# Dealing half of the node blocks over the turns of the gather passes of a graph network

## The chip, the cores and the metric

The kernel runs on one core of one Trainium2 chip. Five engines work beside one another, each through its own instructions in order: TensorE (PE), VectorE (DVE), ScalarE (ACT), GpSimd (POOL) and SyncE (SP), which here only issues transfers. They meet through semaphores. The metric is the device time of one execution, in microseconds (us); lower is better. Before the change three runs took 4184.45, 4190.33 and 4193.7 us.

## The reference, cut to what matters

There are 100,000 nodes of 128 features and 25,000 edges sorted by target. Four graph layers follow one another, each with a layer norm of its residual sum. The last one is a Chebyshev layer in two convolutions, with a ReLU between them. Cut to its chain:

```python
x = _layernorm(x + _L0_gnn_ref(x, edge_attr, ...))       # segment sum of edge attributes, two matmuls, softplus
x = _layernorm(x + _L1_gnn_ref(x, edge_weight, ...))     # own rows @ W_self.T + mean of neighbours @ W_neigh.T
x = _layernorm(x + _L2_gnn_ref(x, w_s, w_n, ...))        # relu(x @ w_s + sum of neighbours @ w_n)
x = _layernorm(x + _L3_gnn_ref(x, W1, b1, W2, b2, ...))  # h = relu(cheb(x)); cheb(h); lap() gathers edges twice in each
```

With so few edges most nodes are nobody's target. A node without an incoming edge goes through the four layers by dense arithmetic alone. The nodes that are targets need gathered rows of their sources at each layer.

## The kernel before, in words

**Stages.** Ten stages follow one another, and at each border every engine drains, adds to the semaphore `seam` (`leave`) and waits for all five (`enter`). They are a preparation (degrees, folded weights, a node table), `tgt0` and `src0` (the first layer for the rows of edge targets and the dense path for the rows of edge sources), `nodes`, then the five gather passes `L1`, `L2`, `T1`, `T2`, `LH`, and a last pass `LU`, which scatters the corrected rows over the output.

**The stage nodes** takes all 100,000 rows in 196 blocks (`BLOCKS`) of 512 rows, each held as 128 partitions by 4 by 128 values, through the four layers without neighbours. Its turn `g` works on six blocks at different depths. SP loads `xin` (`x_load`). POOL adds a constant row (`make_y0`, L599) and looks up two columns of a node table with two indirect transfers (L647). PE transposes `y0` (L1383), multiplies it by `A1` (L1527), and DVE makes `y1` of it (L1023). PE transposes `y1`, multiplies by `ws_sb` (L1533), DVE makes `u2` (L1037). POOL makes `x3 = (u2 - mean) * rs` in four instructions (L622) and `x3b = x3 + gb2_row` in one (L609). PE transposes `x3`, multiplies it by `G02` (L1547), ACT makes the hidden rows `hT` with ReLU (L1273), PE multiplies by `V02` (L1540), DVE adds `x3b` to get `y3` (L1043), and ACT normalizes it into `outb` (L1307), which SP stores. DVE takes moments with `bn_stats` and `bn_aggr` (L969, L974) of `y0`, `u2` and `y3`; ACT takes square roots (L1142) and the sums of squares of `y1` (L1286), and carries the transposed tiles from PSUM to SBUF (L1137).

**A gather pass** has 49 turns (`QUADS`), each over 512 edges: POOL gathers their source rows with four indirect transfers (L563), ACT weighs them, PE transposes them (`sums`, L1401), DVE adds up runs of equal targets with a scan (L853), and PE multiplies the result by the weights of that layer (`first`, `second`). `L1` and `L2` end with a layer norm on DVE; `T1`, `T2` and `LH` are the three steps of the Chebyshev layer. The sums have two PSUM banks, and the products another two to four.

**What orders the work** is the written order of instructions on each engine, and the waits written into it; nothing is planned at run time. In both programs all loops are unrolled.

Of the kernel before, what the change touches and what calls it, by code (L numbers as in the profile page):

```python
# [12 lines left out]
P = 128  # L28
# [14 lines left out]
RING = 4  # L43
assert TILES == 4 * QUADS and QUADS % 2 == 1 and BLOCKS % 2 == 0

# [64 lines left out]
def gnn_kernel(nc, x, src, dst, attr, ew, W1, b1, W2, b2, Wself, bself, Wneigh, bneigh, ws, wn, G1, gb1, G2, gb2, out):  # L110
    ctx = ExitStack()
    with ctx:
# [54 lines left out]
        xin, y0, y1, u2, x3, x3b, outb = (sb(n, [P, 2, 4, P]) for n in ("xin", "y0", "y1", "u2", "x3", "x3b", "outb"))  # L167
# [10 lines left out]
        lk = sb("lk", [P, 2, 4])  # L178
# [4 lines left out]
        pre_in = (y0, x3b, xin, outb)  # L183
# [9 lines left out]
        SELF, NEIGH = (5, 3), (7, 6)  # L193
        HALVES = ((6, 7), (3, 5))
        FIRST = (5, 7)

# [11 lines left out]
        LATE = {"tgt0": 3, "L1": 1, "L2": 1, "T1": 1, "T2": 1, "LH": 1, "LU": 1}  # L208
# [5 lines left out]
        def transfer(name, at_once=2, **n):  # L214
# [6 lines left out]
        x_in = transfer("x_in", nodes=1)  # L221
        xe_in = transfer("xe_in", RING, L1=1, L2=1, T1=1, LH=1, LU=1)
        pre_arrived = transfer("pre_arrived", RING, T2=1)
# [4 lines left out]
        look_in = transfer("look_in", nodes=2)  # L228
        out_st = transfer("out_st", tgt0=1, src0=1, nodes=1)
        oe_st = transfer("oe_st", RING, L1=1, L2=1, T1=1, T2=1, LH=1)  # L230
        more_st = transfer("more_st", src0=1, T1=1, T2=1, LH=1)
# [5 lines left out]
        x3b_made = signal("x3b_made", "nodes")  # L237
# [3 lines left out]
        y3_made, bn3, mv3, rs3, off3_made, looked_up = (  # L241
            signal(n, "nodes") for n in ("y3_made", "bn3", "mv3", "rs3", "off3_made", "looked_up"))
# [11 lines left out]
        out_made = signal("out_made", "tgt0 nodes L1 L2 LH LU")  # L254
# [4 lines left out]
        sd1, h_kept = signal("sd1", "src0"), signal("h_kept", "src0 T2")  # L259
        sd3 = signal("sd3", "nodes")  # L260
        hidden = signal("hidden", {"nodes": 2, "T2": 1})
# [7 lines left out]
        y0_turned, p1_made, y1_turned, p2_made, x3_turned, h_made = (  # L269
            signal(n, "src0 nodes") for n in ("y0_turned", "p1_made", "y1_turned", "p2_made", "x3_turned", "h_made"))  # L270
# [6 lines left out]
        h_turned = signal("h_turned", "T2")  # L277
# [44 lines left out]
        spb, = (yTc[:, n, :] for n in range(1))  # L322
# [3 lines left out]
        LOADS, EDGE_LOADS = 15, 12  # L326
        COUNTED = [c for c in range(TILES) if c % 3 == 0]
        PUT = [c for c in range(TILES) if c % 3 != 0]
        V_COLS, V_WEIGHTS, V_BTC, V_TABLE = 1, 2, 3, 4
        T_TURNED, T_FOLDED, T_A1, T_COUNTED = 1, 2, 3, 4  # L330
# [5 lines left out]
        def _(sp):  # L336
# [6 lines left out]
            with nc.allow_non_contiguous_dma("edge lists with an edge per partition; columns of biases"):  # L343
# [15 lines left out]
                for t, s in ((b1_col, b1), (bs_col, bself), (bn_col, bneigh)):  # L359
                    load(t[:, :], s.rearrange("(p a) -> p a", a=1))  # L360
# [16 lines left out]

            def edge_pass(p, state=None, store=None):
                def state_load(g):
                    if state is None or not g.inside(QUADS):  # L380
                        return
                    if p in ("L1", "T1"):
                        turned.wait(sp, p, g, back=RING)
                    if p == "L2":
                        step.wait(sp, p, g, back=RING)
                    if p == "LH":
                        out_made.wait(sp, p, g, back=RING)
                    if p == "LU":
                        step.wait(sp, p, g, back=RING, k=2)
                    sp.dma_start(xe[:, g.r], quad_of(state, g)).then_inc(xe_in.of(g), 16)  # L390

                def more_load(g):
                    if not g.inside(QUADS):
                        return
                    if p == "T2":
                        pre_added.wait(sp, p, g, back=RING)
                        sp.dma_start(flat(pre_in[g.r]), one(h_pre, g)).then_inc(pre_arrived.of(g), 16)
                    if p == "LU":
                        step.wait(sp, p, g, back=2, k=3)
                        sp.dma_start(gb_in[:, g.b], quad_of(state3, g)).then_inc(x3_in.of(g), 16)  # L400

                def turn(g):
                    state_load(g.less(-3))
                    more_load(g.less(-3 if p == "T2" else -1))
                    g = g.less(LATE[p])
                    if not g.inside(QUADS):
                        return
                    if p == "T1":
                        lap_kept.wait(sp, p, g)
                    elif p == "T2":  # L410
                        near_kept.wait(sp, p, g)
                    elif p != "LU":
                        out_made.wait(sp, p, g)
                    if store is not None:
                        sp.dma_start(quad_of(store, g), oe[:, g.r]).then_inc(oe_st.of(g), 16)
                    if p == "T1":
                        pre_kept.wait(sp, p, g)
                        sp.dma_start(one(h_pre, g), hb[:, g.b].rearrange("p k d -> p (k d)")).then_inc(more_st.of(g), 16)
                    if p == "T2":
                        h_kept.wait(sp, p, g)  # L420
                        sp.dma_start(quad_of(state_h, g), hb[:, g.b]).then_inc(more_st.of(g), 16)
                    if p == "LH":
                        u_kept.wait(sp, p, g)
                        sp.dma_start(quad_of(lap2, g), y1[:, g.b]).then_inc(more_st.of(g), 16)

                enter(sp, p)
                for c in range(3):
                    state_load(Turn(c))
                for c in range(3 if p == "T2" else 1):
                    more_load(Turn(c))  # L430
                run_turns(QUADS, LATE[p], turn)
                if store is not None:
                    oe_st.wait_all(sp, p)
                if p in more_st.n:
                    more_st.wait_all(sp, p)
                leave(sp)

# [58 lines left out]
            def x_load(g):  # L496
                if g.inside(BLOCKS):
                    y0_made.wait(sp, "nodes", g, back=2)
                    sp.dma_start(xin[:, g.b], block_of(x, g)).then_inc(x_in.of(g), 16)

            def nodes_turn(g):
                x_load(g.less(-2))
                g5 = g.less(5)
                if g5.inside(BLOCKS):
                    out_made.wait(sp, "nodes", g5)
                    if g5.c == BLOCKS - 1:
                        out_st.wait(sp, "nodes", g5, back=1)
                    sp.dma_start(block_of(out, g5), outb[:, g5.b]).then_inc(out_st.of(g5), 16)

            enter(sp, "nodes")  # L510
            x_load(Turn(0))
            x_load(Turn(1))
            run_turns(BLOCKS, 5, nodes_turn)
            out_st.wait_all(sp, "nodes")
            leave(sp)

            edge_pass("L1", state1, store=state2)
            edge_pass("L2", state2, store=state3)
            edge_pass("T1", state3, store=lap1)
            edge_pass("T2", store=near_out)  # L520
            edge_pass("LH", near_out, store=most_out)
            edge_pass("LU", most_out)

# [1064 lines left out]
```

## Time and profile before

| | |
|---|---|
| timed runs, us | 4184.45, 4190.33, 4193.7 |
| profiled execution, span from first to last instruction, us | 4620.6 |
| busy PE, DVE, ACT, POOL in that span, us | 3327.5, 3081.8, 2499.0, 3172.0 |
| mean granted clock of TensorE | 0.861 |
| stage nodes, us from the start | 1072 to 2481 |
| the five gather passes, us from the start | 2481 to 4055 |
| last pass, us from the start | 4055 to 4621 |

The times give no separate figure for the profiled execution, so its span stands for its own time. It lies 430 us above the median of the three runs, which were taken without a profile. So a share of what the profile shows is not in the metric, and which share is a question of its own. Busy time of TensorE is modelled at its end points; a gap between two instructions of an engine is shown in brackets with what released the engine.

### The profile page before, as it was taken

The page shows a single profiled execution, that of the slowest core. Times are in us where ns is not written, and L with a number is a line of the kernel's source. Part 1 is how long each engine was busy: PE and PEld are TensorE (multiplying, and loading weights), DVE is VectorE, ACT ScalarE, POOL GpSimd, SP SyncE. Part 2 cuts the span into 40 slices and gives each one's busy share as a digit, 9 for nine tenths or more (in the row PEclk, how much of TensorE's full clock was granted, in tenths as well). Part 3 has the DMA queues.
Part 4 walks back from the last instruction along what each step waited for, and adds up shares of the span by engine and source line. Part 5 has one row for each costly group of instructions (what it writes and reads, how often), then busy time and mean ns, then how long its engine had stood idle before and what let it go on. Part 6 is the DMA issues. An engine that isn't in the chain of part 4 may idle for free.

```text
span 4620.6 us, 74892 instructions
## 1 busy us (share of the span) xinstructions
PE 3327.5 (72%) x20670; PEld 2626.7 (57%) x20670; DVE 3081.8 (67%) x12829; ACT 2499.0 (54%) x7360; POOL 3172.0 (69%) x3630
## 2 busy tenths in 40 slices
PE   2278977778999999999995665658878878821111
PEld 0135646666888888888884654654446667721111
DVE  2298979997888888888885775761224434554454
ACT  0005768996888888888884552115546633311110
POOL 6506668876888888888885665656656646567676
PEclk6598989998999999999997787878989989955555
DMA  0005645662222222222222443435657756632222
GB/s 21 4 1 173 184 133 182 215 216 97 79 75 79 75 79 75 79 75 79 75 79 77 130 131 107 137 123 195 226 192 267 268 195 211 206 109 89 87 91 70
DMA packets 311878, 575.84 MB, mean 125 GB/s; under 512 B 69502, under 2 KB 97975, under 8 KB 311466
## 3 DMA queue, kind: packets, MB, share of 16 engines
q1 hardware_dynamic: 235178, 443.56, 28.5%
q0 software_dynamic: 76288, 127.51, 10.3%
q8 instruction: 171, 2.80, 0.3%
q14 instruction: 241, 1.97, 0.1%
HBM read 301.23 MB, written 271.14 MB: 124 GB/s over the span
## 4 chain that ended last, share of the span: by engine, by line
DVE 42%; issue 17%; PE 15%; another core or an unknown queue 11%; POOL 7%; ACT 5%; DMA 1%; DVEq 0%; SPq 0%; POOLq 0%; ACTq 0%; PEldq 0%; PEld 0%
DVE bn L969 11%; DVE y L1023 5%; DVE mv L974 4%; PE ps L1444 4%; POOL rows L563 3%; DVE u L1037 3%; DVE y L1043 3%; DVE x L853 2%; POOL out_dram L678 2%; PE ps L1383 2%; DVE bn L861 2%; DVE x3b L853 1%; PE ps L1401 1%; PE ps L1462 1%
## 5 line engine op out<-in xcount | busy, mean ns | idle before, releaser
L563 POOL DMA_INDIRECT rows<-state,rows_of_src x588 | 555.8, 945 | 378.6 <-issue 161.7
L853 DVE TENSOR_TENSOR_SCAN x<-same,x,ps 128x512 f32<-128x512 uint8 x336 | 428.8, 1276 | 303.8 <-remote 176.4
L1401 PE MATMUL ps<-ident,rows 128*128 128x128 f32 x1372 | 288.9, 317 | 438.6 <-ACT rows L1154 239.5
L1137 ACT ACTIVATE yTa<-ps 128x512 f32<-128x512 f32 x392 | 232.9, 594 | 567.7 <-PE ps L1383 295.5
L563 POOL DMA_INDIRECT rows<-lap,rows_of_lap x392 | 383.4, 978 | 210.1 <-issue 110.3
L1401 PEld LDWEIGHTS ps<-ident,rows 128*128 128x128 f32 x1372 | 203.6, 166 | 492.0 <-issue 304.7
L647 POOL DMA_INDIRECT lk<-node_table,look_idx x392 | 388.5, 991 | 91.9 <-issue 82.2
L1154 ACT ACTIVATE rows<-rows,lap_w 128x128 f32<-128x128 f32 (+1 forms) x784 | 269.8, 419 | 287.1 <-DMA rows<-lap,rows_of_lap 232.0
L1142 ACT ACTIVATE sd<-mv,consts 128x4 f32<-128x4 f32 x588 | 174.6, 297 | 438.7 <-DVE mv L865 163.8
L1540 PE MATMUL ps<-V,hT 128*128 128x128 f32 x3136 | 405.1, 283 | 8.4 <-ACT hT L1273 8.4
L969 DVE BATCH_NORM_STATS2 bn<-y 128x6 f32<-128x128 f32 x1764 | 378.7, 276 | 23.2 <-POOL y L599 23.1
L1540 PEld LDWEIGHTS ps<-V,hT 128*128 128x128 f32 x3136 | 367.6, 193 | 45.7 <-ACT hT L1273 42.0
L622 POOL TENSOR_SCALAR x<-u,negm,rs 128x128 f32<-128x128 f32 x784 | 339.5, 441 | 72.5 <-issue 61.3
L1547 PE MATMUL ps<-yTc,G 128*128 128x512 f32 x784 | 369.3, 593 | 1.9 <-ACT yTc L1137 1.9
L599 POOL TENSOR_TENSOR y<-xin,c0h 128x512 f32<-128x512 f32 x245 | 311.1, 1270 | 38.3 <-DMA xin<-in_x_dram 28.6
L1307 ACT ACTIVATE outb<-y,off,rs 128x128 f32<-128x128 f32 x784 | 322.5, 491 | 6.6 <-DVE off L999 6.6
L1383 PE MATMUL ps<-ident,x 128*128 128x128 f32 x1372 | 233.2, 298 | 124.3 <-DVE y L949 115.6
L1383 PEld LDWEIGHTS ps<-ident,y 128*128 128x128 f32 x1960 | 232.6, 143 | 148.8 <-issue 131.3
L1527 PE MATMUL ps<-A,yTa 128*128 128x128 f32 x1960 | 283.4, 288 | 34.2 <-ACT yTa L1137 24.1
L1286 ACT ACTIVATE unused<-y 128x128 bf16<-128x128 f32 x980 | 289.6, 310 | 0.0
L1383 PE MATMUL ps<-ident,y 128*128 128x128 f32 x1960 | 260.0, 276 | 38.8 <-POOL y L599 36.3
L1023 DVE SCALAR_TENSOR_TENSOR y<-ps,rs,b1c 128x128 f32<-128x128 f32 x980 | 276.0, 344 | 13.8 <-issue 2.6
(269 smaller groups left out, 9346.5 us busy)
## 6 DMA issues: line engine op xcount, KB each, us to landing
state_h<-hb SPq DMA_DIRECT2D x98, 512.0 KB
xin<-in_x_dram SPq DMA_DIRECT2D x196, 256.0 KB
out_dram<-outb SPq DMA_DIRECT2D x196, 256.0 KB
xe<-state SPq DMA_DIRECT2D x147, 256.0 KB
state<-outb SPq DMA_DIRECT2D x98, 256.0 KB
state<-oe SPq DMA_DIRECT2D x98, 256.0 KB
h_pre<-hb SPq DMA_DIRECT2D x49, 512.0 KB
rows<-in_edge_attr_10x_dram SPq DMA_DIRECT2D x48, 320.0 KB
```

The costliest lines, as they stand in the source:

```text
L563: gp.indirect_dma_start(out=dest[:, at, k, 0:width], out_offset=None, in_=table_, in_offset=bass.IndirectOffsetOnAxis(ap=index[:, c:c + 1] ...
L599: gp.tensor_tensor(y0[:, g.b], xin[:, g.b], all4(c0h[:, :]), ALU.add).then_inc(y0_made.sem, 1)
L622: i = gp.tensor_scalar(x3[:, g2.b, k, :], u2[:, g2.b, k, :], negm[:, g2.b, k:k + 1], rs[:, 2, g2.b, k:k + 1], ALU.add, ALU.mult)
L647: gp.indirect_dma_start(out=lk[:, g.b, 2 * j:2 * j + 2], out_offset=None, in_=node_table, in_offset=bass.IndirectOffsetOnAxis(ap=look_idx[ ...
L853: v.tensor_tensor_scan(t[0:np_, g.b].rearrange("p k d -> p (k d)"), same[0:np_, 512 * g.c:512 * g.c + 512], ps[0:np_, bk + g.b, :], t[0:np ...
L969: i = v.bn_stats(bn[:, n, k, :], y[:, k, :])
L1023: i = v.scalar_tensor_tensor(y1[:, g.b, k, :], bank(3)[:, k, :], dev(0, g.b, k), b1c[:, :], ALU.mult, ALU.add)
L1307: i = a.activation(outb[:, g5.b, k, :], y3[:, g5.b, k, :], ACT.Identity, bias=off3[:, g5.b, k:k + 1], scale=rs[:, 3, g5.b, k:k + 1])
L1383: i = t.transpose(bank(bk)[:, k, :], source[:, k, :], ident[:, :])
L1401: i = t.transpose(bank(g.b)[:, k, :], rows[:, g.r, k, 0:P], ident[:, :])
L1540: i = t.matmul(bank(7)[:, k, :], hT[:, j, k, :], V02[:, j, :], start=j == 0, stop=j == 1)
L1547: i = t.matmul(ps[:, 5 + j, :], G02[:, j * P:(j + 1) * P], yTc[:].rearrange("p k d -> p (k d)"), start=True, stop=True)
```

## The change

- The stage `nodes` handles only the first 98 blocks (`ALONE`). Each block's work on each engine is cut into three parts (`PARTS`): part 0, 1 and 2 of turn `g` are the numbers `3g`, `3g+1`, `3g+2`. In `nodes` the parts run one after another.
- The other 306 parts are dealt over the five gather passes. Four run at each border, before the engines wait for `enter` (on POOL between the first gathers). The 57 or 58 others of a pass run one after nearly each turn, on every engine (`Plan.after`). 286 of them are dealt over the 49 + 2 to 4 turns of the passes, four to seven turns of a pass having two.
- A gather pass keeps one PSUM bank for sums instead of two, one or two for products, and one for transposes, and the dealt parts share banks 0, 4, 5 and 6. Each pass lags its steps by more turns (`TAIL`).
- POOL no longer scales `u2`. DVE makes `x3 = u2 * rs + gb2_row` in four `scalar_tensor_tensor` instructions, and the mean is taken out by multiplying with centred weights (`G02c`), with a corrected bias column (`gb1c_col`). `negm` and the copy of the looked-up columns fall away on DVE. The look-ups (two columns for each of the 98 blocks) write `looked` directly.
- The four-deep ring `xin`, a few new tiles, two small matmuls and one load in the preparation.

The constants, and the parts on VectorE where it matters here:

```diff
+ALONE = BLOCKS // 2
+PARTS = 3
+SHARE = {"L1": 57, "L2": 57, "T1": 57, "T2": 57, "LH": 58}
...
+                if part == 0:
+                    if g.inside(n):
                         y0_made.wait(dve, p, g)
                         stats(0, y0[:, g.b], bn0)
+                    if g1.inside(n):
+                        p2_made.wait(dve, p, g1)
+                        y1_made.wait(dve, p, g1)
+                        v.scalar_tensor_tensor(u2[:, g1.b], bank(4), 0.0, y1[:, g1.b], ALU.max, ALU.add)\
+                            .then_inc(u2_made.sem, 1)
...
+                if part == 2:
+                    if g1.inside(n):
+                        sd2.wait(dve, p, g1)
...
+                        for k in range(4):
+                            i = v.scalar_tensor_tensor(x3[:, g1.b, k, :], u2[:, g1.b, k, :], dev(2, g1.b, k), gb2_row[:, :],
                                                        ALU.mult, ALU.add)
```

Between these, part 0 goes on with the moments of `y0` and `u2`, part 1 makes `y1` of the block `g` and takes the moments of the `y3` of block `g3`, and part 2 ends with `y3` of block `g2`. On ScalarE, parts 1 and 2:

```diff
+                if part == 1:
+                    if g1.inside(n):
+                        root(p, g1, sd2, tv2, sd[:, 2, g1.b, :], tmpv[:, g1.b, :], EPS2)
+                    if g2.inside(n):
+                        p3_made.wait(act, p, g2, back=1)
+                        for j in range(2):
+                            h_made.wait(act, p, g2, k=j + 1)
+                            a.activation(hT[:, j], bank(5 + j), ACT.Relu, bias=gb1c_col[:, j:j + 1])\
+                                .then_inc(hidden.sem, 1)
                     if g3.inside(n):
+                        root(p, g3, sd3, mv3, sd[:, 3, g3.b, :], mv[:, 2, g3.b, :, 1], EPS1)
+                if part == 2:
+                    if g4.inside(n):
+                        off3_made.wait(act, p, g4)
...
+                        i.then_inc(final_made.sem, 1)
+                    if g.inside(n):
+                        keep(p, g, y1T_kept, y1_turned, [(p2_made, 1)], yTb[:, :, :], 0 if shared else 1)
```

The `outb` instructions (L1307 before) stand at the dots of part 2. Part 0 copies the transposed `y0` and `x3` out of PSUM, takes the sums of squares and one root. Every gather pass deals the parts, on each engine, as here on VectorE:

```diff
+                for q in PLAN.seam[p]:
+                    node_part(q)
                 enter(dve, p)
+                for c in range(QUADS + TAIL[p]):
+                    turn(Turn(c))
+                    for q in PLAN.after(p, Turn(c)):
+                        node_part(q)
+                leave(dve)
```

On PE the parts are: part 0 transposes `y0` and the `x3` of two blocks back and multiplies the last block's `y1` by `ws_sb` (in the stage `nodes` the two transposes come first); part 1 multiplies `y0` by `A1` and the `x3` of two blocks back by `G02c`; part 2 transposes `y1` and multiplies `hT` by `V02`.

## Rows read from the trace of the kernel before

**Rows 1.** By stage: us, busy PE, PEld, DVE, ACT, POOL, clock, DMA share, GB/s.

```profile
1072.00:2481.00 1409.00, 1380.15 (x9408) 1133.40 (x9408) 1219.89 (x7272) 1193.63 (x3921) 1214.41 (x1568) 0.99 0.25 75
2481.00:2800.00 319.00, 192.75 (x1176) 179.48 (x1176) 215.75 (x735) 162.62 (x490) 184.94 (x196) 0.78 0.40 122
2800.00:3109.00 309.00, 187.17 (x1176) 174.47 (x1176) 214.26 (x735) 43.09 (x98) 186.35 (x197) 0.79 0.41 126
3109.00:3418.00 309.00, 251.75 (x980) 139.74 (x980) 62.64 (x49) 167.73 (x392) 184.49 (x196) 0.93 0.63 209
3418.00:3730.00 312.00, 255.42 (x1568) 196.79 (x1568) 118.21 (x98) 179.37 (x343) 184.91 (x196) 0.94 0.72 248
3730.00:4055.00 325.00, 255.99 (x1960) 242.94 (x1960) 152.20 (x147) 107.96 (x245) 185.28 (x196) 0.88 0.63 199
```

**Rows 2.** Busy time in the middle of the stage nodes.

```profile
1400.00:1854.00 454.00, 454.00 (x3119) 373.64 (x3118) 399.27 (x2402) 394.76 (x1299) 401.48 (x520) 1.00 0.25 77
```

**Rows 3.** Timeline of PE in nodes: start, us, what, count.

```profile
1800.08 1.14 PE L1527 MATMUL ps<-A,yTa 128*128 128x128 f32 x8
1801.05 1.11 PE L1533 MATMUL ps<-ws_sb,yTb 128*128 128x128 f32 x8
1802.16 2.05 PE L1540 MATMUL ps<-V,hT 128*128 128x128 f32 x16
1804.05 1.88 PE L1547 MATMUL ps<-yTc,G 128*128 128x512 f32 x4
1805.77 1.04 PE L1383 MATMUL ps<-ident,y 128*128 128x128 f32 x8
1806.64 0.60 PE L1383 MATMUL ps<-ident,x 128*128 128x128 f32 x4
1807.08 1.14 PE L1527 MATMUL ps<-A,yTa 128*128 128x128 f32 x8
```

**Rows 4.** Timeline of DVE in the same block.

```profile
1802.51 0.18 DVE L1014 RECIPROCAL rs<-sd 128x4 f32<-128x4 f32 x1
1802.72 1.13 DVE L1023 SCALAR_TENSOR_TENSOR y<-ps,rs,b1c 128x128 f32<-128x128 f32 x4
1803.77 0.68 DVE L1037 SCALAR_TENSOR_TENSOR u<-ps,y 128x512 f32<-128x512 f32 x1
1804.96 0.86 DVE L969 BATCH_NORM_STATS2 bn<-u 128x6 f32<-128x128 f32 x4
1808.10 0.38 DVE L974 BATCH_NORM_AGGREGATE mv<-bn 128x2 f32<-128x6 f32 x4
```

**Rows 5.** Timeline of ACT in the same block.

```profile
1799.41 0.60 ACT L1137 ACTIVATE yTa<-ps 128x512 f32<-128x512 f32 x1 [0.75 <-PE ps L1383]
1800.17 0.30 ACT L1142 ACTIVATE sd<-mv,consts 128x4 f32<-128x4 f32 x1 [0.17 <-DVE mv L974]
1804.01 1.64 ACT L1307 ACTIVATE outb<-y,off,rs 128x128 f32<-128x128 f32 x4
```

**Rows 6.** A group of POOL in the stage nodes: busy us, mean ns, idle before.

```profile
L599 POOL TENSOR_TENSOR y<-xin,c0h 128x512 f32<-128x512 f32 x196 | 248.9, 1270 | 28.7 <-DMA xin<-in_x_dram 28.6
```

**Rows 7.** Timeline of POOL at the border of L1 and L2.

```profile
2800.05 0.94 POOL L563 DMA_INDIRECT rows<-state,rows_of_src  x1 [25.22 <-SPq L291]
2801.30 0.94 POOL L563 DMA_INDIRECT rows<-state,rows_of_src  x1 [0.30 <-issue]
```

**Rows 8.** Waits of POOL in L1, then L2 (total us, times, longest).

```profile
POOL rows L563 <- remote: 19.7, 10, 3.6
POOL rows L563 <- remote: 38.3, 20, 3.7
```

**Rows 9.** Timeline of L2 around one of these waits.

```profile
2950.32 0.69 DVE L940 SCALAR_TENSOR_TENSOR y<-ps,xe 128x512 f32<-128x512 f32 x1 [2.03 <-remote]
2950.61 0.94 POOL L563 DMA_INDIRECT rows<-state,rows_of_src  x1 [1.64 <-remote]
```

**Rows 10.** Timeline of PE in T1 behind a gap.

```profile
3231.72 1.79 PE L1444 MATMUL ps<-yTa,G 128*128 128x512 f32 x2 [1.86 <-issue]
```

More of the change, by code:

```diff
@@ L376, in _ @@
             leave(sp)
[L378 to L436, printed above, removed]
@@ L497, in x_load @@
                 if g.inside(BLOCKS):
[L498 to L508, printed above, removed]
+                    y0_made.wait(sp, "nodes", g, back=RING)
@@ L510, in _ @@
             enter(sp, "nodes")
[L511 to L514, printed above, removed]
+            for c in range(3):
+                x_load(Turn(c))
+            for q in range(PARTS * ALONE):
+                node_part(q)
             leave(sp)
[L517 to L520, printed above, removed]
@@ L652, in _, with merged_pass, rows_of @@
+            assert TILES == 2 * ALONE
             enter(pool, "nodes")
             make_y0("nodes", Turn(0))
-            run_turns(BLOCKS, 4, row_pass("nodes", BLOCKS, look))
+            for q in range(PARTS * ALONE):
+                node_part(q)
             leave(pool)
-            def edge_pass(p, table_, index, width=P):
+            def merged_pass(p, table_, index, width=P):
+                def rows_of(g):
+                    if g.inside(QUADS):
+                        gather(p, g, table_, index, rows, g.r, width, rows_in, [(summed, RING)])
@@ new lines, in squares, with node_part @@
+            def squares(p, g):
+                y1_made.wait(act, p, g)
+                tv2.wait(act, p, g, back=2)
+                squared.wait(act, p, g, back=1)
+                for k in range(4):
+                    i = a.activation(unused[:, k, :], y1[:, g.b, k, :], ACT.Square, accum_out=ssum[:, g.b, k:k + 1])
+                i.then_inc(squared.sem, 1)
+            enter(act, "src0")
+            run_turns(QUADS, 5, src0_turn)
+            leave(act)
+            def node_part(q):
+                p, n = "nodes", BLOCKS
+                g, part = Turn(q // PARTS), q % PARTS
+                g1, g2, g3, g4 = (g.less(k) for k in (1, 2, 3, 4))
+                shared = q >= PARTS * ALONE
+                if part == 0:
@@ L1523, in turn @@
-                    if g.inside(n):
-                        y0T_kept.wait(pe, p, g)
-                        y1_made.wait(pe, p, g, back=1)
-                        for k in range(4):
-                            i = t.matmul(bank(3)[:, k, :], yTa[:, k, :], A1[:, :], start=True, stop=True)
-                        i.then_inc(p1_made.sem, 1)
+                    if not shared:
+                        third_turned()
                     if g1.inside(n):
@@ L1531, in turn @@
                         u2_made.wait(pe, p, g1, back=1)
-                        for k in range(4):
-                            i = t.matmul(bank(4)[:, k, :], yTb[:, k, :], ws_sb[:, :], start=True, stop=True)
-                        i.then_inc(p2_made.sem, 1)
-                    if nodes and g4.inside(n):
-                        hidden.wait(pe, p, g4)
-                        y3_made.wait(pe, p, g4, back=1)
+                        if shared and g3.inside(n):
+                            y3_made.wait(pe, p, g3)
```

982 lines of the change are left out of this document (706 added, 276 removed).

## The prediction

> **What bounds the kernel now.** I read the stages first, then one stage's timeline, then the waits.
>
> The busy times by stage [rows 1] split the part that changes into the stage nodes, 1409 us, and five gather passes of 309 to 325 us, 1574 us together; the sum is 2983 of the 4620.6 us of the profiled span. What lies around it (preparation, `tgt0`, `src0`, `LU`: 1638 us) stays, but for some microseconds of folded weights.
>
> In the stage nodes PE is busy for all of a stretch of 454 us, DVE for 399, ACT for 395, POOL for 401 [rows 2]. The reader is to see in the timeline of PE [rows 3] that each group starts as the one before ends its issue, and that the same product comes back after 7.00 us (1800.08 to 1807.08). So a block costs 7.00 us and PE sets it: 0.97 us for the product with `A1`, 1.11 with `ws_sb`, 1.89 with `V02`, 1.72 with `G02`, 1.31 for twelve transposes.
>
> In a gather pass POOL sets the pace. A gather follows the last after 1.25 us [rows 7], so 196 take 245 us; the border costs 25.2 us [rows 7]; in L2 another 38.3 us are waits whose releaser the profile doesn't know [rows 8]. That is 308.5 of 309 us. PE is busy 187 to 256 us there, DVE 63 to 216 [rows 1]: the room that the change wants to use. What PE needs in it follows from the counts [rows 1] at the prices of [rows 3] (a transpose 0.109 us, a 128-column record 0.118, a 512-column record 0.43). A turn of L1 or L2 has 8 transposes and 16 records, 2.8 us, 136 us a pass. T1 has 12 and 8 wide ones, 4.75 us, 233; T2 12, 4 wide and 16, 4.9 us, 241; LH 8 and 32, 4.65 us, 228.
>
> **The stage nodes after.** The work of PE on a block is the same, 7.00 us. DVE has 6.16 us per block now (399.27 of 454 [rows 2]). Two small instructions go, some 0.1 us, and four `scalar_tensor_tensor` come. The trace has none that reads SBUF alone; the nearest is L1023, 4 in 1.05 us from start to start and 1.13 long [rows 4], against 0.86 for four moments. I take 1.05 and keep 0.86 and 1.13 for the range. With about 0.1 us at five places where DVE waits for its own result (0.21 us from L1014 to L1023 [rows 4], half of it the first one's slot) DVE needs 7.6 us.
>
> But the written order closes a ring that is longer. `u2` starts when the product with `ws_sb` is done. On DVE follow `u2` 0.68, moments of `y0` 0.38, of `u2` 0.86 and 0.38, a small one 0.1, `rs` and `y1` 0.21 and 1.05, moments of `y3` 0.86 and 0.38 [rows 4]: 4.9 us. Only then can ACT take the root of `y3`'s variance, 0.17 and 0.30 us, and behind it in ACT's order stand `outb`, 1.64 us, and the copy of the transposed `y1`, 0.60 [rows 5]. The next product with `ws_sb`, 1.11 us [rows 3], waits for that copy, and the next `u2` for the product. The ring is 8.7 us; neighbours that don't wait overlap a little (y1 is 1.13 long and is followed after 1.05), so I take 8.6. 98 blocks make 843 us, with 12 us, some one and a half loops, for filling and for the index arithmetic at the end, 855. Bounds are PE's 7.00 (698 us) and the ring with a collision or a slow clock (rivals). Here the change costs 1.6 us a block, 157 us, against 98 blocks at 7.00.
>
> What POOL gives up is worth nothing in this stage: it was busy 401 of 454 us behind PE. With four look-ups at the price of a gather (1.25 us [rows 7]) and the sum with the constant row (1.27 [rows 6]) it has 6.3 us a block, under the 8.6.
>
> A rule speaks against the new `x3` as well. The Trainium skill, page "SBUF — State Buffer", section "SBUF: two separate sides", says that a VectorE instruction with two SBUF inputs and a GpSimd instruction that reads SBUF exclude each other on one pair of ports for a whole instruction. No row shows it here, because DVE has no such instruction in the stage nodes now; the sum above goes without it, and it is the fifth case below.
>
> **The gather passes after.** 61 or 62 parts a pass are 20.3 blocks: PE 142 us, DVE 154 us (7.6 each). Added to DVE's busy time [rows 1] and PE's need above:
>
> L1: DVE 216 + 154 = 370, PE 278. L2: DVE 214 + 154 = 368, PE 278. T1: PE 233 + 142 = 375, DVE 217. T2: PE 383, DVE 272. LH: PE 370, DVE 306.
>
> POOL has 245 + 20.3 x 1.27 = 271 us and is no longer the bound; ACT stays below 330 (its busy time in [rows 1] and 6.1 us a block, 394.76 of 454 [rows 2]). The larger of each pass sum to 1866 us. On top:
> - Copies by ACT that PE now waits for, since one bank serves several tiles. In T1 a part 0 has two transposes through one bank, and the copy between them, 0.60 us [rows 5], comes behind T1's own copies: 0.5 us, 20 times. In T2 the weighing of rows stands between two copies: 0.25 us in 49 turns, 0.7 in 20. Together 36 us, 0 to 80.
> - Turns that don't fit. T1's pass now is 25 + 233 + 39 (waits as in [rows 8]) = 297 of 309: 0.25 us a turn is nobody's. 257 turns: 64 us, 0 to 130.
> - Borders and tails. Some 36 parts run there with no edge work between, at a third of 8.6 us rather than of 7.1: 18 us. Of the 25.2 us of a border [rows 7] four parts cover most, since PE has 9 us in them and the first gathered rows come about 14 us after: 5 us each, 25.
>
> The waits that move are SP's: stores of finished blocks now stand in its queue before the loads of the next turn. A load is needed a turn later, 7 us, and I put it at nothing; if it came late, PE's first transposes would wait, at most the 0.75 us that ACT waits for PE in [rows 5] for each turn. The passes come to 2009 us.
>
> **The sum.** 855 + 2009 = 2864 against 2983: 119 us less, by the profile's own time. But the profiled span is 430 us above the median of 4190.33. Where engines abut, as in nodes, I see nothing that a profile could have added. In the passes I do: in the waits without a releaser, 10 to 20 a pass [rows 8], DVE and POOL stand at the same moment, for 2.03 and 1.64 us, and start within 0.3 us [rows 9]. They are 19.7 us in L1, 38.3 in L2 and as much in the other three, 169 us. I take them to be missing in the timed runs. Then the five passes are 1405 us there, nodes and passes 2814, and the change adds 50: 4190 + 50 = **4240 us**, 1.2% slower.
>
> **The cases** (a difference under 0.2%, 8 us, is about what a measurement of this kernel can't tell from none).
> 1. As summed: the slower loop of the lone blocks eats what the overlap gives. 4240, by the bounds of the added waits 4205 to 4310. Chance 0.42.
> 2. The waits of [rows 8] are in the timed runs too, and the fuller passes hide them, because PE and DVE have other work ready. Then the gain is 119 us: 4071, faster. For it: they are waits of engines that depend on gathers. Against: DVE waits in them for nothing that a gather makes, and some 250 us of the 430 would have to be found elsewhere. It decides from 111 us of them on, two thirds. Chance 0.20.
> 3. The ring is not closed, because ACT reaches the copy of `y1` earlier than I think; DVE's 7.6 us set the loop. 98 us less: 4142, faster. Each 0.1 us is 10 us; the sign turns at 8.1 us. Chance 0.15.
> 4. PE's gaps slow its clock. In T1, with a granted clock of 0.93 [rows 1], a gap of 1.86 us is followed by a pair of wide records in about 1.7 us where the stage nodes has 0.86 [rows 3, 10], the two levels of 1.2 and 2.4 GHz. In the lone blocks PE idles some 1.6 us of 8.6 in two gaps. If each block has one such slow stretch, 1.7 us longer, the 98 make 167: 4407, slower. Against: the gaps here are shorter, 1.1 and 0.5 us. Chance 0.12.
> 5. `x3` waits each time for POOL's sum with the constant row, 1.27 us [rows 6]: 98 x 1.27 = 124 us, 4364, slower. It needs POOL's sum in part 2; I expect it behind the first moments of part 0, where it gets its buffer. Chance 0.06.
> 6. Gains and losses meet within 8 us of 4190. Chance 0.05.
>
> That the passes stay bound by gathers after all would need POOL's 271 us above 368; I give it no chance of its own.
>
> Faster 0.35, same 0.05, slower 0.60. The range reaches from case 2 to case 4, 4070 to 4400; the likeliest case's own is 4205 to 4310.
>
> **What would show each step right or wrong.** In the stage nodes: ends near 1930 us, and a block of 8.6 us with a gap on PE before the product with `ws_sb` that ACT's copy ends; a period of 7.6 or less makes me wrong. DVE: four `x3` in 0.86 to 1.13 us. In the passes: about 400 us each, DVE nearly full in L1 and L2, PE in T1, T2 and LH, POOL with gaps released by PE or DVE. Borders with under 10 us of idle PE. If the passes take 370 us or less, or again show waits without a releaser while the timed run gains, the sum is wrong in its second half.

## The result and the profile after

The changed kernel takes 4258.39 us (median of four runs, 4255.75 to 4262.03), the kernel before, on the same chip, 4190.05: a ratio of 1.0170, interval 1.0155 to 1.0185, 68 us slower. The profiled execution of the changed kernel has a span of 4256.3 us, so here the profile's time and the timed runs' agree.

The busy times by stage of the changed kernel (columns as in [rows 1]): `nodes`, which begins at 920 us, and the five passes `L1`, `L2`, `T1`, `T2` and `LH`; `LU` takes the rest, 527 us. A pass begins where POOL issues its first gather.

```profile
920.00:1754.80 834.80, 703.74 (x4664) 542.10 (x4664) 733.95 (x3796) 598.98 (x1937) 497.76 (x491) 0.99 0.22 63
1754.80:2133.70 378.90, 298.24 (x2147) 256.34 (x2148) 354.02 (x1534) 272.41 (x892) 211.71 (x216) 0.96 0.40 131
2133.70:2500.80 367.10, 291.54 (x2155) 257.52 (x2154) 349.27 (x1531) 167.28 (x503) 213.62 (x218) 0.96 0.42 135
2500.80:2896.80 396.00, 373.38 (x1952) 252.17 (x1951) 211.73 (x836) 294.99 (x797) 211.73 (x216) 0.99 0.55 190
2896.80:3365.50 468.70, 406.21 (x2553) 308.99 (x2552) 273.01 (x898) 312.09 (x804) 211.03 (x217) 0.97 0.57 189
3365.50:3729.50 364.00, 344.96 (x2807) 321.67 (x2805) 289.66 (x838) 224.72 (x607) 206.55 (x212) 0.98 0.64 202
```

DVE has been busy for 354 of 379 us in `L1` and 349 of 367 in `L2`, PE for 373 of 396 in `T1` and 345 of 364 in `LH`: POOL's gathers no longer pace the passes. `T2` stands out: 469 us, and PE, its fullest engine, has 62 us without work.

One lone block (a block that the stage `nodes` still handles by itself), in the timelines of DVE, ACT and PE of the changed kernel (start, us, line, count, idle before and what ended it), against [rows 3 to 5]:

```profile
1407.49 0.38 DVE L1019 BATCH_NORM_AGGREGATE mv<-bn 128x2 f32<-128x6 f32 x4
1408.32 1.12 DVE L1139 SCALAR_TENSOR_TENSOR x<-u,rs,gb_row 128x128 f32<-128x128 f32 x4
1409.87 0.69 DVE L1150 TENSOR_TENSOR y<-ps,x 128x512 f32<-128x512 f32 x1 [0.35 <-ACT outb L1501]
1411.46 0.69 DVE L1095 SCALAR_TENSOR_TENSOR u<-ps,y 128x512 f32<-128x512 f32 x1
...
1407.90 0.30 ACT L1315 ACTIVATE sd<-mv,consts 128x4 f32<-128x4 f32 x1 [0.99 <-DVE mv L1019]
1408.10 1.63 ACT L1501 ACTIVATE outb<-y,off,rs 128x128 f32<-128x128 f32 x4
1409.64 0.57 ACT L1310 ACTIVATE yTb<-ps 128x512 f32<-128x512 f32 x1
...
1409.50 0.66 PE L1654 MATMUL ps<-ident,x 128*128 128x128 f32 x4
1410.27 1.16 PE L1779 MATMUL ps<-ws_sb,yTb 128*128 128x128 f32 x8
...
1415.11 0.66 PE L1654 MATMUL ps<-ident,y 128*128 128x128 f32 x4 [1.07 <-DVE y L1119]
```

A ring is a closed chain of waits: each step waits for the one before it, and the first step of the next block for the last step of this one, so that a block takes at least the sum of the steps. This is the predicted ring: the last moments on DVE (ended 1407.87), ACT's root (1407.90), `outb`, the copy of the transposed `y1` (ended 1410.21), the product with `ws_sb` (1410.27 to 1411.43), `u2` (1411.46). `x3` starts at 1399.94, 1408.32 and 1416.71, so a block takes 8.38 us. PE stands still ahead of the product with `ws_sb` for only 0.11 us (1410.16 to 1410.27); its long gap, 1.07 us, is at the transposes of `y1`, which wait for DVE. DVE's row for `y3` shows something the prediction did not have: it too waits for `outb`, 0.35 us, since `y3` has two buffers and `outb` reads the one that it writes. Behind it stand the moments of `y0`, and `u2` only then. Two rings through the same stretch of ACT end within 0.1 us of one another.

### The profile page after: what moved, and what is told of

The parts are those of the page before. It is cut to its first block, busy times and chain, and to the rows that moved or that the text cites. A ratio compares the mean times of both kernels' runs of the same rounds, so it can differ in the third digit from the quotient of the medians.

```text
span 4256.3 us, 74138 instructions
## 1 busy us (share of the span) xinstructions
PE 3198.7 (75%) x20676; PEld 2496.8 (59%) x20676; DVE 3308.1 (78%) x13225; ACT 2513.5 (59%) x7409; POOL 2589.6 (61%) x2650
## 4 chain that ended last, share of the span: by engine, by line
DVE 32%; PE 24%; POOL 16%; issue 14%; ACT 9%; DMA 3%; POOLq 0%; SPq 0%; DVEq 0%; ACTq 0%
DVE bn L1014 6%; POOL rows L599 6%; POOL out_dram L716 4%; PE ps L1779 4%; PE ps L1929 4%; DVE y L1119 3%; DVE mv L1019 3%; ACT outb L1501 3%; POOL node_put L587 3%; PE ps L1654 3%; PE ps L1857 2%; PE ps L1944 2%; PE ps L1945 2%; DMA state_h<-hb 2%; DVE u L1095 2%
## 5 line engine op out<-in xcount | busy, mean ns | idle before, releaser
L665 POOL DMA_INDIRECT looked<-node_table,look_idx x392 | 371.5, 948 | 108.6 <-issue 96.6
L1672 PE MATMUL ps<-ident,rows 128*128 128x128 f32 x392 | 102.4, 358 | 423.3 <-ACT rows L1327 409.8
L1857 PE MATMUL ps<-yTc,G02c 128*128 128x512 f32 x784 | 376.5, 603 | 0.0
L1672 PEld LDWEIGHTS ps<-ident,rows 128*128 128x128 f32 x392 | 63.9, 182 | 443.3 <-ACT rows L1327 414.9
L1196 DVE TENSOR_TENSOR_SCAN agg<-same,agg,ps 128x512 f32<-128x512 uint8 x240 | 305.3, 1272 | 22.4 <-PE ps L1893 14.6
L1327 ACT ACTIVATE rows<-rows,lap_w 128x128 f32<-128x128 f32 x196 | 62.6, 389 | 425.4 <-DMA rows<-lap,rows_of_lap 425.4
L1779 PE MATMUL ps<-ws_sb,yTb 128*128 128x128 f32 x1960 | 279.0, 287 | 39.4 <-DVE y L1150 28.4
L1779 PEld LDWEIGHTS ps<-A,yTa 128*128 128x128 f32 x1960 | 247.5, 198 | 82.0 <-ACT yTa L1310 44.3
L1119 DVE SCALAR_TENSOR_TENSOR y<-ps,rs,b1c 128x128 f32<-128x128 f32 x784 | 220.9, 344 | 90.0 <-issue 71.6
L599 POOL DMA_INDIRECT rows<-state_h,rows_of_src x196 | 186.0, 949 | 171.7 <-PE ps L1895 81.0
```

The costliest lines, as they stand in the source:

```text
L599: gp.indirect_dma_start(out=dest[:, at, k, 0:width], out_offset=None, in_=table_, in_offset=bass.IndirectOffsetOnAxis(ap=index[:, c:c + 1] ...
L665: gp.indirect_dma_start(out=looked[:, c, 2 * j:2 * j + 2], out_offset=None, in_=node_table, in_offset=bass.IndirectOffsetOnAxis(ap=look_id ...
L1119: i = v.scalar_tensor_tensor(y1[:, g.b, k, :], bank(4 if shared else 3)[:, k, :], dev(0, g.b, k), b1c[:, :], ALU.mult, ALU.add)
L1196: v.tensor_tensor_scan(t[:, g.b].rearrange("p k d -> p (k d)"), same[:, 512 * g.c:512 * g.c + 512], ps[:, bk, :], t[:, 1 - g.b, 3, P - 1:P ...
L1779: i = t.matmul(bank(bk)[:, k, :], lhs[:, k, :], w[:, :], start=True, stop=True)
L1857: t.matmul(ps[:, 5 + j, :], G02c[:, j * P:(j + 1) * P], yTc[:].rearrange("p k d -> p (k d)"), start=True, stop=True).then_inc(h_made.sem, 1)
```

## The experiments

Edits are against the changed kernel where nothing else is said; "net" is against its 4258 us. The diffs are shortened, and `...` marks what is left out. The runs were not all timed beside one another: the kernel before, timed again beside them, had medians of 4185 to 4190 us, so some 5 us of a net difference mean nothing.

**The kernel before, profiled once more.**

> The kernel before, profiled once more. If the 430 us by which the first profiled span lay over the timed runs were an accident of that execution, the span is now near 4190 us, with nodes still 98 x 2 blocks at 7.0 us (1380 to 1410 us), preparation, tgt0 and src0 together about 920 us as in the changed kernel, and the five passes about 265 to 285 us each without waits that have no releaser. If they belong to every profiled run, the span is again some 10% over the timed runs.

It took 4184.43 us with a span of 4182.6: the 430 us belonged to that one first execution; what made it so long is not shown. Its stages (columns as in [rows 1]):

```profile
920.00:2326.60 1406.60, 1380.11 (x9408) 1133.36 (x9408) 1219.59 (x7272) 1194.28 (x3921) 1212.38 (x1568) 0.99 0.25 75
2326.60:2598.50 271.90, 172.50 (x1176) 161.31 (x1176) 214.95 (x735) 160.87 (x490) 185.31 (x196) 0.84 0.47 143
2598.50:2861.20 262.70, 168.46 (x1176) 150.27 (x1176) 212.55 (x735) 42.71 (x98) 185.87 (x197) 0.89 0.49 148
2861.20:3124.30 263.10, 239.51 (x980) 137.12 (x980) 62.63 (x49) 169.72 (x392) 185.23 (x196) 0.97 0.74 245
3124.30:3392.40 268.10, 243.93 (x1568) 189.64 (x1568) 118.23 (x98) 177.84 (x343) 185.30 (x196) 0.97 0.85 289
3392.40:3656.30 263.90, 231.96 (x1960) 222.93 (x1960) 153.83 (x147) 110.41 (x245) 185.72 (x196) 0.96 0.77 245
```

`nodes` is as in [rows 1]; the five passes are 1330 us, not 1574, and no wait without a releaser is left. So the stages can be set side by side, without the 430 us:

| us | before | no parts in the passes (below) | after | predicted |
|---|---|---|---|---|
| nodes | 1407 | 1672 | 835 | 855 |
| L1 | 272 | 267 | 379 | 370 |
| L2 | 263 | 260 | 367 | 368 |
| T1 | 263 | 338 | 396 | 375 |
| T2 | 268 | 404 | 469 | 383 |
| LH | 264 | 268 | 364 | 370 |
| on top of the passes | | | | 143 |
| sum | 2736 | 3209 | 2810 | 2864 |

Half of the old `nodes` is 703 us, so the slower lone loop costs 132 us (835 - 703). The passes, 1975 us, are 645 us longer than the 1330 of before, for the other 703: they give 58 back. The balance is 74 us, as between the two profiled spans (4256.3 and 4182.6 us), against 68 between the medians.

**All blocks alone: the new loop without the dealing.**

```diff
-ALONE = BLOCKS // 2
+ALONE = BLOCKS + 4
...
-SEAM_PARTS = 4
-SHARE = {"L1": 57, "L2": 57, "T1": 57, "T2": 57, "LH": 58}
+SEAM_PARTS = 0
+SHARE = {"L1": 0, "L2": 0, "T1": 0, "T2": 0, "LH": 0}
... (on POOL the look-ups stay in the first 98 turns)
```

> The changed kernel with all 196 blocks alone and no parts in the passes: the new x3 and the new loop without the merging. Theory (the lone block costs 8.38 us, and the passes without parts cost what they did before, 1330 us in the second profile of before): 196 x 8.38 + 25 = 1667 for nodes, total 920 + 1667 + 1330 + 527 = 4444, so that merging is worth 186 us and the slower lone loop costs 254 to 260. Rival (the passes' own code became dearer: fewer banks, one for sums in place of two): passes above 1400 us, total above 4510.

4660.54 us. `nodes` came as expected (1672 for 1667). The passes did not: 1537 us for 1330. The two rows of `T1` and `T2` in its busy times by stage:

```profile
3118.80:3457.10 338.30, 247.78 (x980) 138.90 (x980) 62.62 (x49) 172.18 (x392) 184.80 (x196) 0.96 0.57 190
3457.10:3861.20 404.10, 271.91 (x1568) 191.38 (x1568) 120.16 (x98) 188.22 (x392) 184.79 (x197) 0.96 0.58 191
```

The rival was right, and its cause shows in the timelines of `T1` without parts, on PE and ACT:

```profile
3255.26 0.63 PE L1655 MATMUL ps<-ident,xe 128*128 128x128 f32 x4 [1.50 <-ACT oe L1311]
3261.70 0.63 PE L1655 MATMUL ps<-ident,xe 128*128 128x128 f32 x4 [1.50 <-ACT oe L1311]
...
3253.36 1.26 ACT L1540 ACTIVATE hb<-ps,gb_col 128x512 f32<-128x512 f32 x2 [2.12 <-PE ps L1930]
3254.52 0.60 ACT L1311 ACTIVATE oe<-ps 128x512 f32<-128x512 f32 x1
```

A turn is 6.44 us. PE waits for the copy of `oe` out of the one bank that all transposes now share, and ACT waits for PE's product before it. Banks were given to the parts, and the pass alternates between the two engines. That the shared bank is the cause is read from these rows; no run gives the pass its banks back.

`T1` costs 75 us more than before and `T2` 136 without a single part in them. In `T2` the bank is only a part of it: from 3480 to 3830 us of this run, 34% of the chain of waits is the landing of the `state_h` stores, some 5.5 to 6.2 us each, which the runs on `T2` below take up. With the parts the two passes grow by only 58 and 65 us. In `T1` PE waited 73.3 us for the copy of `oe` without parts, in 47 waits; in the changed kernel none of PE's waits there is for it: parts run in that time.

**The lone loop, first try: the copy ahead of `outb`.**

```diff
+ if not shared: keep(p, g, y1T_kept, ...)      # ACT, part 2
  ... outb of g4 ...
- keep(p, g, y1T_kept, ...)
+ if shared: keep(p, g, y1T_kept, ...)
```

> The changed kernel, with ACT's copy of the transposed y1 ahead of outb in the lone blocks alone. Theory (the ring through ACT's order sets the lone block): the ring loses 1.55 us and DVE's own 7.6 us set the block; 98 x (8.38 - 7.6) = 76 us less, 4258 to about 4182, DVE in the lone blocks then without idle time. Rival (the block is set by DVE's own work and its handovers, the ring being only beside it): the block stays above 8.2 us and the time within 15 us of 4258. A block of 7.0 would say that PE sets it.

4278.99 us, net +21: both theories miss. The block became longer, 8.63 us (`x3` at 1397.28 and 1405.91). Timelines of its DVE and ACT:

```profile
1407.93 0.69 DVE L1150 TENSOR_TENSOR y<-ps,x 128x512 f32<-128x512 f32 x1 [0.83 <-ACT outb L1503]
...
1405.69 0.58 ACT L1310 ACTIVATE yTb<-ps 128x512 f32<-128x512 f32 x1
1406.16 1.64 ACT L1503 ACTIVATE outb<-y,off,rs 128x128 f32<-128x128 f32 x4
```

The edit took `outb` out of one ring and put the copy into the other, the one through the buffers of `y3`. DVE's wait there rose from 0.35 to 0.83 us.

**`outb` early: at the start of part 1 on ACT.** Its inputs are there since the part before.

```diff
 if part == 1:                                 # ACT
+    if not shared: outb of g4                 # was in part 2
     root(p, g1, sd2, ...)
     relu of hT, root(p, g3, sd3, ...)
```

> The changed kernel, with outb of a lone block at the start of part 1 on ACT (its offsets are there since the part before) in place of part 2. The run with the copy first only exchanged one ring for another: y3 waits for outb, since it writes the buffer that outb reads, and outb stood behind the root that waits for DVE's last moments. Theory: with outb behind neither, no ring through ACT is longer than DVE's own work; the block falls from 8.38 to DVE's 7.5 to 7.7 us, 98 blocks make 65 to 85 us, total 4175 to 4195. Rival (another wait of DVE, for PE's third product or ACT's relu of hT, which outb now delays by 1.5 us, closes a ring of the same length): 8.2 us or more, total within 20 us of 4258.

4229.61 us, net -29, the block 8.09 us (`x3` at 1406.95 and 1415.05). It lies between the two expectations. Timelines of its DVE and PE:

```profile
1409.80 0.69 DVE L1095 SCALAR_TENSOR_TENSOR u<-ps,y 128x512 f32<-128x512 f32 x1 [0.28 <-PE ps L1785]
...
1413.45 0.66 PE L1660 MATMUL ps<-ident,y 128*128 128x128 f32 x4 [1.08 <-DVE y L1119]
1414.04 2.05 PE L1882 MATMUL ps<-V,hT 128*128 128x128 f32 x16
1415.93 0.60 PE L1660 MATMUL ps<-ident,y 128*128 128x128 f32 x4
1416.36 0.60 PE L1660 MATMUL ps<-ident,x 128*128 128x128 f32 x4
1416.80 1.06 PE L1785 MATMUL ps<-ws_sb,yTb 128*128 128x128 f32 x8
```

No row of DVE waits for `outb` now, but a third ring is closed: PE waits for `y1`, does five steps in its written order (transposes of `y1`, product with `V02`, transposes of `y0` and of `x3`, product with `ws_sb`), and `u2` waits for the last.

**T2: the relu of `hTm` ahead of the copy of `oe` on ACT.**

```diff
 rows_kept(g2, 1)
+pre_added.wait(act, p, g1); relu of hTm[g1.b]
 product.wait(act, p, g2); copy to oe[:, g2.r]
-pre_added.wait(act, p, g1); relu of hTm[g1.b]
```

> The changed kernel, with ACT's relu of hTm ahead of the copy of oe in T2 alone. Theory (T2 goes back and forth between PE and ACT through one bank; ACT idles 2.14 us a turn for the second product while the relu's input is there): the relu's 1.05 us fits into that wait, 49 turns make 51 us; T2 468 to about 418 us, total about 4208. Rival (the landing of the state_h stores, 5.3 us of 25 in the chain of waits, sets T2): T2 and the total stay within 10 us of 468 and 4258.

4241.50 us, net -17; `T2` 448 us in place of 469. ACT's waits for the second product fell as they should, in the stretch of `T2` from 109.7 to 54.7 us in 49 waits, but only 20 of the 51 us came through. The chain of waits of this run still holds, once in two turns (pieces under 0.05 us are left out):

```profile
3010.77 1.23 DVE hTm L1254
3012.03 0.32 SPq L486
3012.39 5.62 DMA state_h<-hb
3018.03 0.60 ACT hb L1546
```

The store of `state_h` is issued behind the load of L486 in SP's queue, which waits for DVE's sum; ACT can refill `hb` only when the store has landed, 5.62 us later.

**T2: that edit, and the store ahead of the load on SP.**

```diff
+if p == "T2" and g3.inside(QUADS):
+    h_kept.wait(sp, p, g3); sp.dma_start(quad_of(state_h, g3), ...)
 state_load(g.less(-early))
...
-    h_kept.wait(sp, p, g3); sp.dma_start(quad_of(state_h, g3), ...)
```

> The changed kernel with ACT's relu ahead of the copy of oe in T2, and in SP's turn of T2 the store of state_h ahead of the load of h_pre (which waits for DVE's sum). Relu alone gave 17 us of the 51 expected; the chain of waits still has a landing of state_h, 5.6 us, once in two turns of 8.2 us, issued right behind that load. Theory (the store waits for DVE's sum only by its place in SP's queue): the landing leaves the chain, 20 to 24 of them at some 2 us each net or more, T2 448 to 400 to 425 us, total 4195 to 4220. Rival (the PE and ACT alternation is as long by itself): T2 stays at 440 or more, total 4235 or more.

4226.37 us, net -32; `T2` 435 us, between the two expectations again. The landing is gone from the chain of waits. What is left in it, turn after turn, are ACT's two copies out of the shared bank and PE's second product, with the weighing of rows and the parts between them: the alternation seen in `T1`.

**Borders: no parts in the last turns, eight parts between passes in place of four.**

```diff
-SEAM_PARTS = 4                # SHARE 57, 57, 57, 57, 58
+SEAM_PARTS = 8                # SHARE 53, 53, 53, 53, 54
-n = QUADS + TAIL[p]
+n = QUADS
```

> The changed kernel, with no parts in the last turns of a pass and eight parts in place of four between two passes (the middle has as many parts a turn as before). Theory (DVE leaves a pass late, some 8 us after the last store, because parts stand in its last turns, and next gathers wait for it): each of the five borders gets 5 to 12 us shorter, 25 to 60 us in all, 4200 to 4235. Rival (the borders are bound by the landing of the last stores and by the flight of the first rows, and parts there cost what they cost elsewhere): within 12 us of 4258.

4285.57 us, net +27. From first gather to first gather `L1` took 384.7 us, `L2` 378.0, `T1` 404.8, `T2` 474.3: 6 to 11 us more each, `LH` 363.1. Both theories miss. The run changes two things at once, the parts in the last turns and the number of parts between passes, so it doesn't tell which of them cost the time, nor what sets a border.

**The two edits together** (`outb` early, and the pair of edits on `T2`), with `outb` early in the passes too.

```diff
-    if not shared: outb of g4                 # ACT, part 1
+    outb of g4
```

> The two edits above together, with outb at the start of part 1 in the passes too. If both theories hold: 4258 less 76 and less 45, 4137 (4110 to 4170), under the 4189 of the kernel before. If only the lone loop's holds: about 4180; if only T2's: about 4210; if neither: 4240.

4196.44 us (ratio to before 1.0025, 1.0014 to 1.0036). The measured parts add up: 4258 - 29 - 32 = 4197.

**On top of these: the product with `ws_sb` first on PE, and the same with the reciprocal behind `x3` on DVE.**

```diff
 if part == 0:                                 # PE
+    if not shared: products(p2_made, g1, 4, yTb, ws_sb)
     turn4(y0), turn4(x3)
-    if not shared: products(p2_made, g1, 4, yTb, ws_sb)
```

```diff
 if part == 2:                                 # DVE, the second kernel alone
-    sd3.wait(dve, p, g3); reciprocal to rs[:, 3, g3.b, :]
     x3 of g1
+    sd3.wait(dve, p, g3); reciprocal to rs[:, 3, g3.b, :]
```

> The kernel with the edits together, and on PE in a lone block the product with ws_sb ahead of the transposes of y0 and x3. With outb early the lone block measured 8.09 us: u2 to the end of y1 on DVE 3.6 us, then on PE the transposes of y1, the product with V02, eight transposes and the product with ws_sb, 4.5 us. Theory (this DVE and PE ring now sets the block): it loses the eight transposes' 0.87 us; DVE, with one wait of 0.30 for ACT's root left, sets 7.8 us; 98 x 0.27 = 27 us, 4196 to 4170. Rival (DVE and its handovers need 8.1 us by themselves): within 8 us of 4196.

> The same, and on DVE the reciprocal of y3's deviation behind x3 in place of ahead of it, so that ACT has 1.1 us for the root. Theory: DVE then stands nowhere for another engine in a lone block, 7.5 us; 98 x 0.57 = 56 us less than with the edits together, 4196 to 4140, under the 4185 of the kernel before by 1%. Rival (a ring through another engine is again about 7.8 or more): 4165 or more.

4262.77 and 4267.50 us: 66 and 71 more than without. The lone block is 8.77 us in both. Timelines of PE and ACT of the first:

```profile
1404.45 2.05 PE L1884 MATMUL ps<-V,hT 128*128 128x128 f32 x16 [0.84 <-ACT hT L1502]
...
1407.87 0.60 ACT L1310 ACTIVATE yTa<-ps 128x512 f32<-128x512 f32 x1 [2.80 <-PE ps L1658]
1410.19 1.64 ACT L1481 ACTIVATE outb<-y,off,rs 128x128 f32<-128x128 f32 x4
1411.92 1.25 ACT L1502 ACTIVATE hT<-ps,gb1c_col 128x512 f32<-128x512 f32 x2
```

The copy of `y0` now waits for a later transpose, and behind it ACT has `outb` ahead of the relu for which PE's product with `V02` waits, and so the next transposes: a fourth ring.

**`outb` behind that relu**, against the second of these.

```diff
 if part == 1:                                 # ACT
-    outb of g4
     root(p, g1, sd2, ...), relu of hT
+    outb of g4
     root(p, g3, sd3, ...)
```

> The last kernel (product first, root later, 8.77 us a lone block) with outb behind the relu of hT in place of ahead of it. Its ring was ACT's copies, squares, outb 1.54 us and relu, then PE's product with V02, the product with ws_sb and the transposes of y0: 8.77 us. Theory: the ring loses outb's 1.54 us and is 7.2; the DVE and PE ring is 7.1; DVE's own work, 7.5 to 7.7 us, sets the block; 98 x 1.1 = 108 us less than 4267, 4160 (4140 to 4185), under the kernel before. Rival (yet another ring of 8 us or more): 4195 or more.

4228.37 us, the block 8.14 us (`x3` at 1399.77 and 1407.91): the rival. The chain of waits goes through `outb`, the root, the copy of `y1`, PE, the copy of `y0`, the relu, and `outb` again: a fifth. `T2` was 455 us here, 21 more than with the two edits together; why is open.

**Deeper buffers for `y3`, and every ring that was found under 7.3 us by the measured durations.**

```diff
-y3 = sb("y3", [P, 2, 4, P])
+y3 = sb("y3", [P, RING, 4, P])
-final_made.wait(dve, p, g2, back=2)
+final_made.wait(dve, p, g2, back=RING)
```

With it ACT has the copy of `y1` ahead of `outb` and the relu of `hT` ahead of the root for `x3`, PE the product first, DVE the reciprocal behind `x3` and `tmpv` behind `y1`, and `T2` its two edits.

> All rings found so far cut at once. T2's two edits; y3 in four buffers in place of two, so that DVE waits for outb only four blocks back; on ACT the copy of y1 ahead of outb, and the relu of hT ahead of the root for x3; on PE the product with ws_sb first; on DVE the reciprocal behind x3 and the small row of the variance behind y1. Theory (each arrangement so far met a ring through one-deep tiles, 8.38, 8.63, 8.09, 8.77, 8.14 us, above DVE's 7.6 us of work): no ring above 7.3 us is left by the measured durations, the block is 7.6 to 7.7 us and the lone blocks take 72 us less than in the changed kernel, T2 33 less; 4258 to 4153 (4135 to 4175), under the 4187 of the kernel before. Rival (one more ring of 8 us or more, or the shared parts suffer by the new order): 4195 or more.

4175.01 us, ratio to before 0.9971 (0.9962 to 0.9980): slightly faster than the kernel before, and 83 us under the changed one. A lone block takes 7.73 us. Timelines of its DVE and ACT:

```profile
1405.12 0.38 DVE L1019 BATCH_NORM_AGGREGATE mv<-bn 128x2 f32<-128x6 f32 x4
1405.63 0.18 DVE L1108 RECIPROCAL rs<-sd 128x4 f32<-128x4 f32 x1
...
1405.31 0.29 ACT L1315 ACTIVATE sd<-mv,consts 128x4 f32<-128x4 f32 x1
```

No row of DVE carries a bracket, and yet one waits. The reciprocal for `y1` starts 0.13 us after the moments end (1405.50), and 0.03 us after ACT's root ends (1405.60). The chain of waits shows what stands behind it (pieces under 0.05 us are left out, longer ones where `...` stands):

```profile
1405.63 0.19 DVE rs L1108
...
1407.03 0.66 PE ps L1655 x4
1407.68 1.85 PE ps L1881 x16
1409.53 0.89 PE ps L1780 x8
1410.42 0.45 PE ps L1655 x4
...
1411.39 0.59 ACT yTc L1310
1411.98 1.16 ACT unused L1464 x8
1413.14 0.20 ACT sd L1315
1413.36 0.19 DVE rs L1108
```

That is a sixth ring, of 7.73 us and not under 7.3: DVE makes `y1`, PE transposes it, multiplies by `V02` and by `ws_sb` and transposes the next `y0`, ACT copies it, takes the sums of squares and the root, and DVE's next `y1` waits for that root. DVE is busy for 370.8 of 386.5 us (1200.00 to 1586.50, 50 blocks), 7.42 us a block; with its waits for its own results its work comes to some 7.6 us. So this ring lies only 0.13 us above it.

`nodes` gave 58 us (`L1` begins at 1697.2 for 1754.8), where 72 were expected, and `T2` 30 (439 us) for 33; together they are the 88 us between the two profiled executions. The medians differ by 83, so the total is 22 us over the expectation.

## Why the prediction was right, and where not

- **Direction and size.** 4240 for 4258, inside the likeliest case's own range of 4205 to 4310, and by that case's mechanism: the lone loop loses more than the passes win. The prediction's sum has some 150 us lost and 100 won (the passes grow from 1405 to 2009 us for 704 us of blocks); measured it is 132 against 58 us. That the difference came so close, 50 for 74, is in part luck: see the point on the profile's 430 us.
- **The lone block.** 8.6 predicted, 8.38 measured, 855 and 835 us for the stage. The ring was named with its steps, and each step's rows are there. Its sign was read a little wrong: the gap on PE ahead of the product with `ws_sb` is 0.11 us, and the long one is elsewhere. What the prediction missed is that this ring is not the only one: orders that cut it gave 8.63, 8.09, 8.77, 8.14 and at last 7.73 us, each set by another ring.
- **DVE's 7.6 us, and case 3.** The work was right: some 7.6 us of a block of 7.73. The case's condition, ACT reaching the copy earlier, was wrong as a way there: run by itself it made the block longer. Of the 98 us that the case promised, five changes of order and one deeper tile brought 64 by the block (98 x 0.65), 58 by the stage.
- **`x3`.** Four in 1.04 to 1.05 us up to the start of what follows, 1.05 taken.
- **The passes.** `L1`, `L2` and `LH` lie within 9 us of the fuller engine's sum, `T1` 21 above. In the three, two errors cancel: the fuller engine is busy 354, 349 and 345 us where the sum had 370, 368 and 370, and idle for 25, 18 and 19 us, about what a fifth of the waits for unfit turns and borders comes to (107 us in all). The 143 us on top came out as 109 (1975 - 1866), but 86 of them in `T2`. The term that was mis-sized is the copies by ACT that PE waits for, 36 us with 80 as the upper bound, all of it in `T1` and `T2`: these two lie 107 us above the sum. Their own new code costs 211 us without a part (75 + 136); in `T1` the rows show waits between PE and ACT at the shared bank, in `T2` the landing of `state_h` beside them, and the parts hide much of both. A loss of that kind I had not priced at all. SP's order was put at nothing for another reason, stores of finished blocks ahead of loads; what the runs found is a store behind a load that waits, 13 us in `T2` (448 to 435).
- **Borders.** Under 10 us of idle PE holds between `L1` and `L2` (4.3 of the 40 us from 2120 on) and between `T2` and `LH` (7.9 of the 40 from 3350 on); in the other two it is 12.3 and 10.1 (from 2485 and from 2880 on). What sets a border is open.
- **The profile's 430 us.** I took 169 of them out of the passes. The second profile of before has 244 less in the passes (1574 to 1330). So both sides of the sum were too high, after by 54 us and before by 78, and the errors largely cancelled. That the 1638 us around the change stay was wrong for the same reason: they are 1447 in the second profile of before and as many after. The 4205 to 4310 take the bounds of the added waits one at a time; both together (0 to 80 and 0 to 130 us) give 4140 to 4350. Case 2 was said to decide from 111 us on; by its own sum 58 us, a third of the 169, would do (50 and 8).
- **The other cases.** Case 2 (waits that the passes hide): they are in no other profile. Case 4 (a slow clock behind gaps): the granted clock in `nodes` is 0.99 after as before, and the products keep their 1.06 us. Case 5 (a shared port): exclusions are there, but in few blocks, see below. That DVE had no instruction with two SBUF inputs in `nodes` before is not quite so: two small ones of 128x4 stand there (L1061, 0.18 us, and L999, 0.13).

## What to carry to other kernels

Merging two loops moves the price into buffers: count what each side loses in PSUM banks and tile depth, and run the merged code once with the guests left out; here that showed some 207 us which no sum of busy times had. In a loop that is one block ahead, list all rings through shared tiles and orders before cutting the longest, since its neighbours lie within some tenths of a microsecond. Making a tile deeper takes a wait away without putting another instruction later; here it was run only together with five changes of order, so its own share is not known. A row without a marked wait may still wait, for 0.13 us here: compare its start with the end of what it reads. And profile the baseline twice before anything is worked out from one span.

## What the runs showed of the hardware that was not expected

A profiled span can be some 440 us too long for the kernel it shows: 4620.6 us once and 4182.6 the next time, with timed runs of 4184 to 4194. Its cause is open. The excess lay in the passes (244 us) and in the stages around (191 us), not in `nodes`, which kept its 1407 to 1409 us.

In the changed kernel 5 of the 196 groups of four `x3` coincide with POOL's sum with the constant row; the other 191 take 1.13 us in the mean, these 2.41 to 2.95. The first of them, timelines of POOL and DVE:

```profile
945.28 1.28 POOL L635 TENSOR_TENSOR y<-xin,c0h 128x512 f32<-128x512 f32 x1
...
945.16 2.41 DVE L1139 SCALAR_TENSOR_TENSOR x<-u,rs,gb_row 128x128 f32<-128x128 f32 x4
```

POOL keeps its 1.28 us, and DVE's group is longer by as much (1.13 + 1.28 = 2.41). In the other four it is 2.79 to 2.95 us, longer by 1.7 to 1.8, more than POOL's instruction; that difference is open. The Trainium skill, page "SBUF — State Buffer", section "SBUF: two separate sides", says that the two exclude each other on a shared pair of ports for a whole instruction; the trace agrees as far as DVE's waits of at least POOL's 1.28 us show it. It cost little, some 8 us in all, because in nearly all blocks POOL's sum runs at another time: in the lone loop it starts behind the first moments of `y0` (1411.51, those ended 1411.34), as the prediction expected.
